# A six-stage decoder on one core: 194 TensorE matmuls on an identity, whose results nothing reads, are left out

## The reference, cut to what matters

```python
x = _layernorm(x + _L0_attn_ref(x, ...))               # causal self-attention
x = _layernorm(x + _L0_xattn_ref(x, ..., ctx, ctx, 8)) # long convolution against the context
x = _layernorm(x + _L0_ffn_ref(x, ...))                # ternary weights, quantised activations
x = _layernorm(x + _L1_attn_ref(x, ...))               # linear recurrence
x = _layernorm(x + _L1_xattn_ref(x, ctx, ...))         # cross-attention, 16 heads, 4 of keys and values
x = _layernorm(x + _L1_ffn_ref(x, ...))                # gated feed-forward in fp8
```

## Time and profile before

| | |
|---|---|
| median of 3 runs | 885.41 us (884.24 to 886.17) |
| profiled execution | 885.34 us |
| its span | 883.3 us |
| mean granted TensorE clock in it | 0.979 of full speed |
| TensorE busy | 821.2 us, 93% |
| VectorE busy | 691.8 us, 78% |
| ScalarE busy | 521.6 us, 59% |
| GpSimd busy | 295.5 us, 33% |
| instructions in the trace | 14409 |

### The profile page before, as it was taken

The page is one execution under the profiler, slowest core; times in us unless marked ns, Lnnn a source line. Parts: engine busy times, 40 slices in busy tenths (PEclk is TensorE's granted clock), DMA queues, the critical chain, the costliest instruction groups (busy, mean ns, idle before and its releaser), DMA issues.

```text
span 883.3 us, 14409 instructions
## 1 busy us (share of the span) xinstructions
PE 821.2 (93%) x5004; PEld 640.0 (72%) x5004; DVE 691.8 (78%) x1703; ACT 521.6 (59%) x1299; POOL 295.5 (33%) x315
## 2 busy tenths in 40 slices
PE   6876979799999999999999999999999999999984
PEld 5754756688787777867687777976778777777763
DVE  2696777987899869887897879987898888555654
ACT  4547115546735866387735875269742788667863
POOL 1442713531454226421472124622273134111100
PEclk9898979999999999999999999999999999999999
DMA  8942010010001000100001000010000000000000
GB/s 288 375 133 84 25 25 13 1 24 1 13 1 25 24 13 1 25 13 14 12 1 24 14 13 13 1 37 1 13 1 12 3 1 1 1 13 1 13 1 24
DMA packets 37062, 28.65 MB, mean 32 GB/s; under 512 B 18688, under 2 KB 34560, under 8 KB 36608
## 3 DMA queue, kind: packets, MB, share of 16 engines
q1 hardware_dynamic: 36992, 27.74, 10.2%
HBM read 25.64 MB, written 2.10 MB: 31 GB/s over the span
## 4 chain that ended last, share of the span: by engine, by line
PE 56%; DVE 27%; ACT 7%; issue 6%; DMA 1%; POOL 1%; SPq 1%; DVEq 0%; POOLq 0%; ACTq 0%
PE bank L1328 9%; PE bank L1289 8%; PE bank L1020 5%; PE bank L1307 4%; PE bank L1317 4%; PE bank L1207 4%; PE bank L1121 2%; DVE Zc L768 2%; DVE S L948 2%; PE bank L1312 2%; DVE OT L771 2%; PE bank L1089 1%; PE bank L1091 1%; PE bank L1092 1%; DVE prod L271 1%
## 5 line engine op out<-in xcount | busy, mean ns | idle before, releaser
L651 ACT ACTIVATE S<-S,mx 128x128 f32<-128x128 f32 x256 | 99.4, 394 | 45.2 <-DVE mx L951 44.9
L1289 PE MATMUL bank<-XTE,w_xq 128*128 128x256 f32 x512 | 124.0, 386 | 0.9 <-DVE vq L939 0.5
L1328 PE MATMUL bank<-w_xo,OX 128*128 128x256 f32 x512 | 116.0, 379 | 0.0
L1289 PEld LDWEIGHTS bank<-XTE,w_xq 128*128 128x128 f32 x512 | 95.0, 192 | 17.8 <-issue 3.2
L1328 PEld LDWEIGHTS bank<-w_xo,OX 128*128 128x128 f32 x512 | 95.6, 190 | 14.2 <-issue 1.8
L642 ACT ACTIVATE QS<-bank,per_partition_sb 128x256 f32<-128x256 f32 x128 | 60.7, 474 | 59.1 <-PE bank L1289 55.2
L374 POOL TENSOR_TENSOR rq<-vq,minus_half 128x8 f32<-128x8 f32 x32 | 53.3, 1665 | 118.4 <-DVE vq L939 118.2
L948 DVE SCALAR_TENSOR_TENSOR S<-bank,rq,xmask 128x128 f32<-128x128 f32 x256 | 71.8, 343 | 17.6 <-PE bank L1307 15.6
L1307 PEld LDWEIGHTS bank<-KTX,QA 128*128 128x128 f32 x512 | 63.7, 192 | 10.2 <-issue 8.3
L271 POOL TENSOR_TENSOR prod<-XTA,ccolA 128x256 f32<-128x256 f32 x96 | 59.8, 655 | 30.9 <-PE bank L1092 21.3
L1307 PE MATMUL bank<-KTX,QA 128*128 128x128 f32 x512 | 67.8, 277 | 0.6 <-ACT OX L663 0.6
(11 more groups left out here) (223 smaller groups left out, 1846.3 us busy)
## 6 DMA issues: line engine op xcount, KB each, us to landing
xin<-in_x SPq DMA_DIRECT2D x8, 256.0 KB, 2.7
taps_sb<-in_taps SPq DMA_DIRECT2D x1, 2048.0 KB, 11.5
cnat<-in_ctx SPq DMA_DIRECT2D x8, 256.0 KB, 2.7
ccolA<-in_ctxT SPq DMA_DIRECT2D x32, 64.0 KB, 2.7
ccolE<-in_ctxT SPq DMA_DIRECT2D x16, 128.0 KB, 2.3
w_xq<-in_L_xattn_Wq SPq DMA_DIRECT2D x1, 2048.0 KB, 12.1
w_xo<-in_L_xattn_Wo SPq DMA_DIRECT2D x1, 2048.0 KB, 17.6
out_x<-X SPq DMA_DIRECT2D x8, 256.0 KB, 2.1
```

What stands on the lines that cost most here:

```text
L651: ins = nc.scalar.activation(S[:, b, seq(h)], S[:, b, seq(h)], ACT.Exp, bias=mx[:, b, h:h + 1], accum_out=sm[:, b, h:h + 1])
L1289: ins = nc.tensor.matmul(cols(EQ)[:, h], w_xq[:, k, hh * XDIM:(hh + 1) * XDIM], XTE[:, k], start=k == 0, stop=k == HALVES - 1)
L1328: ins = nc.tensor.matmul(rows(EY)[:, b], OX[:, h, b], w_xo[:, n * XGROUP + h], start=n == 0 and h == 0 and b == 0, stop=n == XKV - 1 and h ...
```

## The change

The helper and its five calls go, with the two waits that stood in front of two of them. The strings of steps stay as they were.

```diff
-            def keep_clock(spare, n):
-
-                for _ in range(n):
-                    nc.tensor.matmul(spare[:, 0:P], ident_bf[:], ident_bf[:], start=True, stop=True)
-
             def front(g):
...
                 sig(ins, "a_sc")
-                if g == 0:
-                    pe.wait_ge(sems["pool_const"], 2)
-                    keep_clock(EY, 24)
                 yield
...
                 sig(ins, "a_y")
-                if g == 0:
-                    keep_clock(EY, 30)
                 yield
...
                 sig(nc.tensor.matmul(A1[:], skip_w[:], SK[:].rearrange("p b d -> p (b d)"), start=True, stop=True), "b_skip")
-                if g == 0:
-                    keep_clock(EY, 24)
                 for u in range(8):
...
                 sig(ins, "b_oT")
-                if g == 0:
-                    keep_clock(EY, 60)
...
                     sig(ins, "e_y")
-                    if g == GROUPS - 1 and n == XKV - 1:
-                        pe.wait_ge(sems["e_vq"], nth(g, XKV, XKV - 1))
-                        keep_clock(EQ, 56)
```

## The result

| | before | changed |
|---|---|---|
| median, 7 runs each | 884.47 us (882.92 to 886.17) | 887.05 us (885.73 to 888.76) |
| ratio of changed to before | | 1.0029, 95% interval 1.0018 to 1.0039 |
| profiled execution, its span | 885.34, 883.3 | 887.05, 885.0 |
| mean granted clock of the profiled execution | 0.979 | 0.968 |

A later comparison with 12 runs of the changed kernel and 23 of the one before gave 1.0033 (1.0020 to 1.0046).

What follows compares the result with a forecast made beforehand. The prediction took TensorE, busy 821.2 of 883.3 us, to bound the kernel. Start -0.7, middle +1.0 and end +1.9 summed to +2.2, added to 885.34 for 887.5 us; range 885.0 to 889.8.

Steps and rivals of the forecast that it cites:

- The sum: Whole kernel: start, middle and end together +2.2 us, giving 887.5 us.
- The blocks as work: All five places: removing the matmuls gives back nothing, except 1.3 us at the 24 before the first taps.
- The second 24: Block right before the first taps: taps start 2.56 us earlier, 1.3 us gained after 24 products, shrinking to 0.7.
- The fall at 23: Start: the clock falls at about 23 us instead of 29.9, slowing transposes and attention output by 1.6 us.
- The chain to the taps: Start: score transposes, attention output and transposes of x at low clock add 1.6 us before the taps.
- The middle: Convolution's end to line 1159: without the 60 the clock falls before 65.4 us; +1.0 us, bounds 0 and +1.6.
- The end: Last group: after a 4.1 us hole, line 1121 starts at half clock; +1.9 us, bounds 0 and +3.8.
- the term of the start: Start up to the first 24 tap products: -0.7 us, bounds -2.6 to +1.6.
- Less to do: Rival, whole kernel: TensorE is the bound and has less work, so faster, 883.1 us; chance 0.09.
- No change: Rival: clock holds at 65 us and returns within the end's first chunk; +0.2, 885.5 us; chance 0.38.
- the much slower case: Rival: full clock prices at start and end together; +4.7, 890.0 us; chance 0.13.
- The sign of being wrong: Wrong if PEclk stays 1.00 over line 1121, or a delay at 70 us is gone by 160 us.

Runs made afterwards that it cites:

- no_third: Kernel before without only the 24 matmuls right before the first taps: ratio 1.0005 (0.9995 to 1.0016).
- no_end: Kernel before without only the 56 matmuls of the last group, compared twice: ratios 1.0002 and 1.0020.
- no_sixty: Kernel before without only the 60 matmuls behind the last turn of the convolution: ratio 1.0000 (0.9987 to 1.0013).
- filled_no_end: Kernel before plus four blocks in long waits and 30 matmuls at 62.9 us, the 24 before the taps moved earlier, the last 56 removed: 0.9975, 882.30 us.
- only_end: Kernel before without the start's four blocks (24, 30, 24, 60), the 56 at the end kept, compared twice: ratios 1.0014 and 1.0021.
- holes: Kernel before plus four more blocks (90, 50, 50, 36 matmuls) in TensorE's longest waits: ratio 0.9958, 881.34 us.
- after_again: The changed kernel once more, against new runs of the kernel before: ratio 1.0033 (1.0020 to 1.0046).
- filled_more: Kernel before plus four blocks in long waits, 30 matmuls at 62.9 us and three short blocks, the 24 before the taps moved earlier: 0.9942, 879.29 us.

## Why the prediction was right, and where its parts were not

*The sum.* +2.2 was forecast, +2.6 measured at the median, +2.2 between the two profiled executions by the marks. (The time of 887.5 is near 887.05 also because the execution that it was added to, 885.34, was 0.9 above the median of the comparison, 884.47.) The mechanism was the forecast one: no gain from the work, a loss from the clock. That the sum fits this well is in part luck: its terms for the start and for the end were off by about 1 us each, in opposite directions (below).

*The blocks as work.* 24, 30 and 56 stood in waits: right, the changed kernel waits 2.72 and 2.22 us where 1.38 and 1.33 were. The 60 too: the wait for VX behind them grew from 0.69 to 1.99. The second 24: with the earlier fall the start gained 0.68 in this pair, 0.7 was forecast. But the 1.3 that the forecast started from holds only with the clock low over the taps; with the clock up, no_third against no_end, the block costs 0.2. I had taken the one traced state of the start as the state of the kernel.

*The fall at 23.* It came at 22.6, the score transposes took 0.66, the output 2.08, the transposes of x 1.11: right. The chain to the taps grew by 1.2 us and not by 1.6, as the skip product waited for GpSimd's SK in any case (0.32 us idle before it), and that took up the 0.4 of the slower transposes. The clock was back at 36.3.

*The middle.* Forecast +1.0 out of 0 to 1.6; +0.8 in the pair. The fall came before 65.4 as said. But four profiles have a fall here with the 60 in place, so the term was charged to blocks that don't reliably prevent it, and no_sixty measures nothing (1.0000, 0.9987 to 1.0013).

*The end.* Forecast +1.9; +2.1 in the three traces in which the low clock lasted 6.8 us (changed twice, filled_no_end) and +1.2 in the two in which it lasted 3.4. In the comparisons, 0.2 and 1.8 us.

*The division between start and end.* Here the term of the start was mis-sized. Start and middle together, the four blocks, were forecast at +0.3; only_end measures +1.2 and +1.9. The end was forecast at +1.9; no_end measures +0.2 and +1.8. The means of each pair, 1.55 and 1.0, add up to 2.6, as the whole does, but more of it lies at the start than I said, and less at the end. How it divides exactly stays open, as the two comparisons of each kernel lie 0.7 and 1.6 us apart. The prediction's own sum was drawn from an execution in which the clock had fallen in spite of the start's blocks, so it could not show what they are worth where it holds.

*The rivals.* "Less to do" has fallen: holes adds 226 matmuls and is faster. "No change" has fallen in both comparisons of the changed kernel. The full prices of the much slower case (1.6 and 3.8) were never seen together; the low clock did not last to the end of the last stage in any trace with a low line 1121. The sign of being wrong, a delay at 70 us that is gone by 160, was not seen, but the pair hardly tested it, with +0.05 at the Q transposes of 83 us and +0.08 at those of 162. In after_again the delay did not stay as it was either: 1.3 became 2.8.

*The rule of the Trainium skill* ("TensorE: Matmul & The Clock Gate", section "Why this matters for your kernels"), that idle gaps between bursts take TensorE back to half rate, carried the forecast, and the trace agrees: 4.1 us with 0.06 of work, and 0.50 behind it. Not every gap does it: with the 60 in place, the gap before the QQ transposes had a fall in it or right behind it in four profiles and none in before and no_end2. The same page's remark in Part 1, that the count of slow matmuls at the start differs from run to run of one kernel, had no row of before for or against it; two traces show it now. Before and no_end run the same instructions up to 860 us. The first four transposes of line 1014 took 1.06 us in before (its length where PEclk is 0.50 is 1.06 to 1.11) and 0.73 in no_end, the eight products of line 987 behind them 2.65 and 1.89. (The windows view shows a PEclk of 1.00 over both, so its value this early, before the first change of the clock in a trace, is not to be trusted.) The later falls differ in the same way, which is more than the remark says: 6.8 us at half before 61 us in one of the two, none in the other.

*Open:* what decides where in an execution the falls land was not tried, so the traces' sizes can't be turned into means without many profiles. Whether the start's four blocks or their single members carry the 1.2 to 1.9 us is open too: the intervals of no_third and no_sixty both hold 1 and reach to 1.0016 and 1.0013.

## What to carry to other kernels

Matmuls that nobody reads can be worth their place: look at the granted clock before taking TensorE's busy time as the thing to save, and at what runs behind each wait. Put such blocks where TensorE waits on others, above all ahead of a dense stretch with nothing beside it; three of the blocks here left 0.9 to 1.4 us of their wait empty, and other lengths were not compared. One trace shows one placing of the falls: with effects of 1 us, take a dozen runs or more, and read the stage's own length between two marks.

## What had not been expected of the hardware

- The same instructions gave a start with 6.8 us at half clock and one with none, and 2.9 us between them at the second taps. The 85 times of the kernel before spread from 882.6 to 887.6 us; with nearly all low stretches gone, the five of filled_more spread from 877.9 to 879.7.
- Runs of one kernel differ in their mean clock, and in time with it: of 85 runs of before the 7 with 0.977 average 886.6 us, the 50 with 0.980 and 0.981 average 884.1.
- A block in one wait need not protect the work behind the next ones: in no_third the clock fell at 870.6, 2.9 us behind the end of the 16 products, with waits of 1.4 and 1.0 us in between. In eight other profiles with the same waits it did not.
